# Ten filter units and most loads of the first spectra moved into the last turns of stage 1, in a three-stage graph-network kernel on one Trainium2 core

## What is computed

```python
h = relu(layernorm(x))                                   # layer 0
x = x + relu((norm_adj @ h) @ W.T + b)
h = relu(layernorm(x))                                   # layer 1
c = relu(bn1(conv1(h)))                                  # kernel width 1
c = bn2(conv2(c))                                        # width 17 along the nodes
x_conv = relu(c + h)
s = h @ w_se.T + b_se                                    # 3 features
A = exp(-|s_n - s_m|^2) * adj
x_nmp = A @ relu(h @ w_msg.T + b_msg)
x = x + GRU([x_conv, x_nmp], h)                          # three gates
```

## Time and profile before

| | us |
|---|---|
| median of 3 runs | 1807.17 (1806.46 to 1809.41) |
| the profiled execution's own time | 1806.71 |
| its span | 1804.9 |
| PE busy | 1770.6 (98%) |
| DVE, ACT, POOL busy | 1213.0, 997.1, 836.5 |

### The profile page before, as it was taken

The page is one execution under the profiler, slowest core; times in us unless marked ns, Lnnn a source line. Parts: engine busy times, 40 slices in busy tenths (PEclk is TensorE's granted clock), DMA queues, the critical chain, the costliest instruction groups (busy, mean ns, idle before and its releaser), DMA issues.

```text
span 1804.9 us, 29811 instructions
## 1 busy us (share of the span) xinstructions
PE 1770.6 (98%) x10214; PEld 1568.7 (87%) x10214; DVE 1213.0 (67%) x2306; ACT 997.1 (55%) x1781; POOL 836.5 (46%) x989
## 2 busy tenths in 40 slices
PE   6999999999999989999999999999999999999998
PEld 5999999999999979999988888888888888888887
DVE  7999999999999825555784544544544545545545
ACT  4888888888888866656542332332332332333322
POOL 5788888887777527656731221221221212212211
PEclk9999999999999999999999999999999999999999
DMA  6566566665555446676973435345345344344442
GB/s 205 173 197 221 197 212 206 201 221 189 200 193 189 153 132 147 166 174 158 226 202 101 85 102 121 81 103 123 78 107 118 77 113 104 87 117 89 101 110 42
DMA packets 513876, 262.56 MB, mean 145 GB/s; under 512 B 365639, under 2 KB 473543, under 8 KB 513726
## 3 DMA queue, kind: packets, MB, share of 16 engines
q1 hardware_dynamic: 513182, 260.58, 52.8%
q10 hardware_dynamic: 544, 0.07, 0.0%
HBM read 151.51 MB, written 109.05 MB: 144 GB/s over the span
## 4 chain that ended last, share of the span: by engine, by line
PE 94%; DVE 2%; issue 2%; POOL 1%; ACT 1%; DMA 0%; SPq 0%; ACTq 0%; DVEq 0%; POOLq 0%
PE P L113 70%; PE P L585 6%; PE P L912 5%; PE P L614 4%; PE P L654 4%; PE P L767 3%; PE P L633 1%; PE P L594 1%; DVE yo L792 0%; DVE wsum L730 0%; POOL axl L550 0%; DMA col<-in_cols 0%; DVE wh0l L742 0%; POOL af L547 0%; DMA yt<-y_d 0%
## 5 line engine op out<-in xcount | busy, mean ns | idle before, releaser
L894 POOL TENSOR_TENSOR xnx1l<-xnf,xnx1h 128x1024 fp32r<-128x1024 f32 x16 | 44.0, 2749 | 336.7 <-ACT xnx1h L887 336.7
L894 POOL TENSOR_TENSOR xnx0l<-xnf,xnx0h 128x1024 fp32r<-128x1024 f32 x15 | 41.6, 2772 | 317.7 <-ACT xnx0h L887 317.7
L1011 ACT ACTIVATE tr<-P,cold 128x512 f32<-128x512 f32 x64 | 44.2, 690 | 194.4 <-PE P L113 194.4
L1014 ACT ACTIVATE nn<-gn,col 128x512 f32<-128x512 f32 x64 | 46.4, 725 | 179.3 <-DVE gn L1035 179.3
L1044 DVE SCALAR_TENSOR_TENSOR tz<-tz,tr 128x512 f32<-128x512 f32 x63 | 43.6, 693 | 145.3 <-ACT tz L1025 145.2
L585 PE MATMUL P<-ah,hd 128*128 128x256 f32 x512 | 123.0, 383 | 12.2 <-ACT hd L383 12.2
L1025 ACT ACTIVATE tz<-P,cold 128x512 f32<-128x512 f32 x63 | 43.4, 689 | 159.6 <-PE P L113 159.6
L547 POOL TENSOR_TENSOR af<-af,at 128x512 f32<-128x512 f32 x64 | 111.0, 1735 | 42.1 <-ACT af L345 40.2
L1031 DVE SCALAR_TENSOR_TENSOR gn<-tr,gn 128x512 f32<-128x512 f32 x64 | 44.9, 701 | 127.3 <-ACT tr L1011 127.3
L550 POOL TENSOR_TENSOR axl<-af,axh 128x512 fp32r<-128x512 f32 x64 | 101.8, 1591 | 55.3 <-ACT axh L363 55.3
L585 PEld LDWEIGHTS P<-ah,hd 128*128 128x128 f32 x512 | 93.8, 192 | 22.7 <-ACT hd L383 12.2
(11 more groups left out here) (200 smaller groups left out, 6402.1 us busy)
## 6 DMA issues: line engine op xcount, KB each, us to landing
xh_d<-xst SPq DMA_DIRECT2D x64, 320.0 KB, 4.5
xl<-xh_d SPq DMA_DIRECT2D x40, 512.0 KB, 6.3
y_d<-yo SPq DMA_DIRECT2D x80, 256.0 KB, 2.5
x<-in_x SPq DMA_DIRECT2D x64, 256.0 KB, 2.7
a<-in_adj SPq DMA_DIRECT2D x64, 256.0 KB, 3.0
at<-in_adjt SPq DMA_DIRECT2D x64, 256.0 KB, 4.2
x_d<-x SPq DMA_DIRECT2D x64, 256.0 KB, 4.5
xn_d<-xt SPq DMA_DIRECT2D x64, 256.0 KB, 4.3
```

The lines of the kernel that those rows point to most:

```text
L894: e.e.tensor_tensor(o[1][:, :, :], xnf[p % 2][:, :, :, :].rearrange("p c i t -> p c (i t)"), o[0][:, :, :], ALU.subtract).then_inc(done, 1)
```

## The change

- PE: units 0 to 9 go into turns 66 to 69: unit 0, 2 and 4 at the end of turns 66, 67 and 68, units 1, 3 and 5 ahead of `dist` in turns 67, 68 and 69, units 6 to 9 at the end of turn 69. Units 0 to 5 share bank AG, each waits for the copy of the one before; from unit 6 on banks 4 to 7 are used as before. DVE makes the ten copies (a new semaphore `wevd`), ACT the others.
- ACT: from turn 66 on `h` comes right behind `msh` instead of behind `xst`. In the passage `xh0h` comes one unit's copy earlier, behind unit 20's.
- SP: the store of a group's spectra is cut by halves of the bins first (a, b) and then by channel, with a semaphore for each half (`sxa0`, `sxa1`, `sxb0`, `sxb1`), and stands ahead of the other stores of its turn. The last group's two a stores are issued in turn 71, its two b stores in turn 72. Four loads of the first 15 of 16 groups, for bin pairs 0 to 3, are issued at the end of turn 68; four small ones for the last group at the end of turn 71, once the a stores have landed.
- `first_stage_done` no longer waits for `sxb1`; ACT and DVE do that a little later (`last_spectra_stored`).
- The buffers `xs`, `a_` and `eye2` are placed where `xl` will lie, so that the early loads overwrite only what turn 68 no longer reads.

Three `nm_d` stores now come behind the four large loads. The diff, cut to its core:

```diff
         def first_sync(e, i):
             ...
                 load_adjt(e, i)
+
+            if live(i, 11, NB - 4):
+                store_spectra(e, i - 11)
+            if NB + 7 <= i < NB + 9:
+                for n in range(2):
+                    store_spectra(e, NB - 4 + 2 * (i - NB - 7) + n)
             ...
-            if live(i, 11, NB):
-                g, c, r = (i - 11) // 4, (i - 11) % 4 // 2, (i - 11) % 2 * NF
         ...
         def first_scalar(e, i):
             ...
+            if i >= NB + 2 and live(i, 6):
+                relu(e, i - 6)
             ...
+            if i < NB + 2 and live(i, 6):
+                relu(e, i - 6)
         ...
         def first_vector(e, i):
             ...
+            for n in UNITS_BEHIND.get(i - 1, ()):
+                unit_out(e, n)
             if live(i, 5):
             ...
                 t.then_inc(S["uv"], 1)
+            for n in UNITS_INSIDE.get(i, ()):
+                unit_out(e, n)
         ...
+        ONE_BANK, EARLY = 6, 10
+        UNITS_INSIDE = {NB + 3: (1,), NB + 4: (3,), NB + 5: (5,)}
+        UNITS_BEHIND = {NB + 2: (0,), NB + 3: (2,), NB + 4: (4,), NB + 5: (6, 7, 8, 9)}
         def filter_unit(e, n):
             ...
-            e.wait_ge(S["wev"], n - 3)
+            if n < ONE_BANK:
+                e.wait_ge(S["aglo"], NB)
+                e.wait_ge(S["wevd"], n)
+            else:
+                for name in ("aglo", "uvf", "xxlo", "tcm0", "tcm1"):
+                    e.wait_ge(S[name], NB)
+                units_out(e, max(n - 3, ONE_BANK))
         ...
+        def load_first_spectra(e):
+            for name in ("x2", "hd", "deg0", "ah"):
+                e.wait_ge(S[name], NB)
+            e.wait_ge(S["sxa0"], 32 * (NG // 2))
+            e.wait_ge(S["sxa1"], 32 * (NG // 2 - 1))
+            for q in range(2):
+                load_groups(e, q, 0, NG - 1)
+        def load_last_spectra(e):
+            e.wait_ge(S["sxa1"], 32 * (NG // 2))
+            for q in range(2):
+                load_groups(e, q, NG - 1, NG)
         ...
+                if i == NB + 4:
+                    load_first_spectra(e)
+                if i == NB + 7:
+                    load_last_spectra(e)
             first_stage_done(e)
-            for q in range(2):
-                load_spectra(e, q)
         ...
-            for n in range(UNITS):
-                if n == UNITS - 4:
+            for n in range(EARLY, UNITS):
+                if n == UNITS - 5:
                     first_stage_done(e)
                     spectra_hi(e, 0)
                 unit_out(e, n)
             ...
             spectra_hi(e, 1)
+            last_spectra_stored(e)
         ...
             weights_lo(e, 0)
+            last_spectra_stored(e)
             weights_sum(e, 1)
         ...
-            for n in range(UNITS + AHEAD):
+            for n in range(EARLY, UNITS + AHEAD):
                 filter_unit(e, n)
```

More of the change, by code:

```diff
@@ L121 @@
 out0 u x2 sx20 sx21 st1 ag1a ag1 rs1 n1b xn xnt xt sxt xxhi xxlo s uvf uvh uv cm0 cm1 tcm0 tcm1 h1 mshi mslo
-dist af am axhi axlo nmp nm snm dft0 dft1 xe0 xe1 sxh0 sxh1
-unit yz wev lxh0 lxh1 xsum xhi xlo wsum whi wlo frq com mt ye sy0 sy1 sy2 sy3
+dist af am axhi axlo nmp nm snm dft0 dft1 xe0 xe1 sxa0 sxa1 sxb0 sxb1
+unit yz wev wevd lxh0 lxh1 xsum xhi xlo wsum whi wlo frq com mt ye sy0 sy1 sy2 sy3
 lwg0 lwg1 lwg2 lwg3 lwg4 lwg5 wghi wg ly0 ly1 ly2 lxn0 lxn1 lnm0 lnm1 nmhi nmlov nmlop xnhi xnlov xnlop
@@ L195, in gnn_kernel @@
         xx = p1.hl("xx", [128, 512])
+        p1.at = spectra_at = keep.at + 40960
+        xs = [p1(f"x{i}", [128, 2, 256]) for i in range(5)]
+        a_ = [p1(f"a{i}", [128, 2, 256]) for i in range(2)]
+        eye2 = p1("eye2", [128, 512])
+        at = [p1(f"at{i}", [128, 512]) for i in range(7)]
+        x2 = [p1(f"x2{i}", [128, 2, 256]) for i in range(2)]
         stage = Place(nc, p1.at)
@@ L270, in load_adjt, with store_spectra @@
                 S[f"lat{b % 2}"], 16)
+        def store_spectra(e, k):
+            g, c, r = k // 4, k % 2, k % 4 // 2
+            e.wait_ge(S[f"xe{c}"], 4 * g + 4)
+            e.e.dma_start(xh_d[g][:, c, 16 * r * NF:16 * (r + 1) * NF],
+                          xst[g % 2][:, c, r * NF:(r + 1) * NF, :].rearrange("p r t -> p (r t)")).then_inc(
+                              S[f"sx{'ab'[r]}{g % 2}"], 16)
         def first_sync(e, i):
@@ L309, in spectrum_out, with relu @@
             e.wait_ge(S[f"dft{c}"], b + 1)
-            e.wait_ge(S[f"sxh{g % 2}"], 64 * (g // 2))
+            for half in "ab":
+                e.wait_ge(S[f"sx{half}{g % 2}"], 32 * (g // 2))
             e.e.copy(dst, src).then_inc(S[f"xe{c}"], 1)
+        def relu(e, b):
+            e.wait_ge(S["tcm0"], b + 1)
+            e.wait_ge(S["tcm1"], b + 1)
+            e.wait_ge(S["dft1"], b - 1)
+            e.e.activation(h1[b % 2][:, :, :], tcm[:, :, 0:256], ACT.Relu).then_inc(S["h1"], 1)
         def first_scalar(e, i):
@@ L577, in first_tensor @@
                 t.then_inc(S["nmp"], 1)
+            for n in UNITS_INSIDE.get(i, ()):
+                filter_unit(e, n)
             if live(i, 2):
@@ L635, in first_tensor @@
                 t.then_inc(S["xnt"], 1)
+            for n in UNITS_BEHIND.get(i, ()):
+                filter_unit(e, n)
         def unit_parts(n):
@@ L666, in unit_out @@
                 dst = wf[part % 2][:, :, c, 7 * j0:7 * (j0 + turns)].rearrange("p r (m o) -> p m r o", m=turns)
-                src = P[4 + n % 4][:, 0:140 * turns].rearrange("p (m r o) -> p m r o", m=turns, r=20)
+                src = P[unit_bank(n)][:, 0:140 * turns].rearrange("p (m r o) -> p m r o", m=turns, r=20)
             else:
                 dst = wf[part % 2][:, :, c, 7 * j0:256]
-                src = P[4 + n % 4][:, 0:140].rearrange("p (r o) -> p r o", r=20)[:, :, 0:parts(j0)]
-            e.e.copy(dst, src).then_inc(S["wev"], 1)
+                src = P[unit_bank(n)][:, 0:140].rearrange("p (r o) -> p r o", r=20)[:, :, 0:parts(j0)]
+            if n < EARLY:
+                e.e.tensor_copy(dst, src).then_inc(S["wevd"], 1)
+            else:
+                e.e.copy(dst, src).then_inc(S["wev"], 1)
         AHEAD = 4
@@ L684, in units_in, with load_groups, spectra_loaded @@
             return range(first + n * m // 18, first + n * (m + 1) // 18)
+        def load_groups(e, q, first, end):
+            for c in range(2):
+                e.e.dma_start(xl[q % 2][:, 16 * c + first:16 * c + end, :],
+                              xh_d[first:end, :, c, 64 * q:64 * q + 64].rearrange("g p r -> p g r")).then_inc(
+                                  S[f"lxh{q % 2}"], 16)
+        def load_first_spectra(e):
[9 more added lines that the diff above has]
+                load_groups(e, q, NG - 1, NG)
         def load_spectra(e, q):
-            for n in range(2):
-                e.wait_ge(S[f"sxh{n}"], 64 * (NG // 2))
+            for name in ("sxa0", "sxa1", "sxb0", "sxb1"):
+                e.wait_ge(S[name], 32 * (NG // 2))
             e.wait_ge(S["xhi"], 2 * q - 2)
             e.wait_ge(S["xlo"], 2 * q - 2)
[L692 to L695, removed]
+            load_groups(e, q, 0, NG)
+        def spectra_loaded(e, f):
+            e.wait_ge(S[f"lxh{f // 2 % 2}"], 32 * (f // 4 + 2))
         def bin_of(f):
```

34 lines of the change are left out of this document (16 added, 18 removed).

## The result

| | before | changed |
|---|---|---|
| median, us | 1806.99 (6 runs, 1805.34 to 1809.41) | 1797.49 (6 runs, 1795.71 to 1797.74) |
| span of the profiled execution | 1804.9 | 1794.6 |

The ratio is 0.9948, interval 0.9939 to 0.9958: faster by 0.5%. The forecast was 1797.5.

The account below looks back on a forecast made before the run. PE was taken to bound the kernel (94% of the chain). Unit 10 earlier (-0.8), 21.19 to 13.5 us of units (-7.6) and the wait (-1.1) sum to -9.5 us: 1797.5 forecast, own range 1796.4 to 1801, with rivals 1795.8 to 1802.0.

Parts of the forecast that it names:

- unit 10: First unit left in the passage after stage 1: starts at 663.0 us with POOL's allowance, against 663.76 before.
- 56 matmuls: PE's units left between stage 1 and stage 2: 13.5 us, where 86 matmuls took 21.19.
- The slots: PE's idle slots in turns 67 to 69: units 0 to 5 mostly fit, turn 69's `dist` about 0.4 us later.
- the gap: PE's 3.13 us idle ahead of the last `nmp`: four units, 2.9 us, hide wholly there.
- the clock: PE's clock behind the last `nmp` stays up; before, low clock cost 1.08 us in `dft` and 0.2 in `nmp`'s tail.
- the wait for `wh0l`: PE's wait ahead of stage 2: 1.38 us becomes 0.3, by 0.4 from ACT catching up and 0.7 from less overlap.
- POOL beside the copies: Turn 69's chain: DVE's unit copies slow POOL by 0.1 us, bounds 0 and 2 x 0.5.
- The moved `h`: ACT's earlier `h` from turn 66 on: ends `tcm`'s 4.43 us wait but doesn't shrink the turn, counted as nothing.
- Rival 1: Early loads delay turn 69's `nm_d` store and so the last `nmp`: 1797.5 to 1800.5 us, chance 12%.
- Rival 2: Last group's small loads land late, `xh0h` starts at 677 instead of 671, some 4 us reach PE: 1801.5, chance 8%.
- Rival 3: Units lengthen turns 67 to 69 instead of filling slots, 4.3 us in all: 1801.8 us, chance 6%.
- Rival 4: SP's new store order delays ACT's copies in 53 turns; at 0.3 us a turn 1813 us, slower, chance 3%.

Follow-up runs that it names:

- e4: Changed kernel with units 6 to 9 back behind stage 1, so PE's gap ahead of the last `nmp` stays open: 1804.01 us, ratio 0.9988.
- e10: e4 plus twelve throw-away matmuls behind turn 69's `dft`, whose results are never read: 1800.07 us, ratio 0.9968.
- e5: Changed kernel with POOL's `xsum` of the second bin pair waiting for DVE's first `wh0l`: 1796.37 us, ratio 0.9941.
- e3: Changed kernel with ACT's `h` back at its old place behind `xst` in all turns: 1798.51 us, ratio 0.9957.
- e2: Changed kernel with all ten units back behind stage 1, early loads and the rest kept: 1806.02 us, ratio 1.0002.
- e7: Changed kernel with the four large loads issued at the end of turn 70 instead of 68: 1803.55 us, ratio 0.998.
- e1: Changed kernel with the loads back behind `first_stage_done`, units staying in turns 66 to 69: 1804.04 us, ratio 0.9987.
- e8: Kernel before with only SP's order changed, each turn's spectra store ahead of its other stores: 1806.91 us, ratio 1.0.
- e11: Changed kernel once more, unaltered: 1796.75 us, ratio 0.9952 against the kernel before.
- e9: Changed kernel with twelve units moved instead of ten, and `xsum` of bin pair 1 behind `wh0l`: 1795.91 us, ratio 0.9938.

## Why the prediction was right

The steps (us). The forecast's times count in the trace of before; taking off that trace's 621.10, and 619.84 from the measured ones, sets both at the `dist` of turn 65:

| step | forecast | measured |
|---|---|---|
| `dist` of turn 69, later by | 0.40 | 0.22 |
| last `nmp`, counted from turn 65's `dist` | 39.30 | 39.26 |
| last `nmp` to unit 10 | 2.5 | 2.60 |
| unit 10, earlier by | 0.8 | 0.80 |
| 56 matmuls | 13.5 | 13.52 |
| wait ahead of stage 2 | 0.3 | 0.77 |
| stage 2, earlier by | 9.5 | 9.08 |

- **The slots, the gap and the clock** came as forecast. In turn 69 two small errors cancel: `dist` came 0.18 us earlier than forecast, and the chain from it to the last `nmp` took 4.89 us, not 4.75. The clock's share was argued from one slow `dft`; e4 and e10 measure it alone as 1.6 us, where the working had 1.08 + 0.2 + 0.5 = 1.8.
- **The mis-sized term is the wait for `wh0l`**: "most of that overlap goes: 0.7" was only 0.50 us of `wh0l`'s length (2.23 to 1.73), and PE's wait fell by 0.61 in all instead of 1.08. `xsum` starts 3.5 us behind `xh0h` in both traces, but `wh0h` 2.96 us behind it instead of 2.48, so `xsum` gained only half a microsecond on `wh0l`. The other piece, 0.4 for ACT catching up before unit 25, was 0.1: `wh0h` starts 2.29 us ahead of the end of PE's units (675.22) instead of 2.17 (684.95). e5 takes the whole overlap away (1.00 us of `wh0l` instead of the forecast's 0.7) and so gets the wait of 0.26 that I had put here, though ACT caught up by less.
- **POOL beside the copies, 0.1**: not needed. `axl` took 1.27 us at 657.57, right beside DVE's four copies (2.74 us from 656.54), and 1.28 at 642.38 with no copy beside it. The rule of the prediction held: the copies read PSUM, and POOL didn't feel them. The same section of the Trainium skill (SBUF — State Buffer, "Who interferes with whom") says that a DVE instruction with two SBUF inputs does contend with a GpSimd instruction that reads SBUF. The trace agrees: `wh0l` reads two tensors in SBUF, and beside `xsum` it lost half a microsecond.
- **The moved `h`, nothing**: the edit alone lengthens the passage by 0.34 us when undone (e3). I had asked what it gains against before, and not what the units would cost without it: part of its worth stood unseen in the slots' term.
- **Rival 1** (`nm_d` behind the loads): the delay was real, 3.7 us to landing instead of 2.0, and larger than forecast. Counted from turn 65's `dist` the store landed at 38.0, where the forecast's 658.5 is 37.4 and its 659.6, the latest time that costs nothing, is 38.5. So 0.5 of the 1.1 us of slack were left. In e2 the same store took 4.8 us, and ACT's `nm` copy did wait for it, by 0.30 us, which PE's wait for `axl` covered. The sign was near, and the forecast's account of it holds by half a microsecond.
- **Rival 2**: the small loads were issued at 665.36 and landed within 1.9 us, so `xh0h` didn't wait. Its mechanism is real, and its price was too small: e7 has `xh0h` 4.2 us late and pays 5.4 us, since the wait of PE was followed by a low clock, there and in e1.
- **Rival 3**: by turn 69's `dist` the turns with units had grown by 0.2 us together. **Rival 4**: e8 shows 0.00 us a turn.
- **The total.** The medians differ by 9.5 us and the passage by 9.08. The start-up alone moves single executions by over a microsecond, so there is luck in 1797.49 for 1797.5 (the same kernel gave 1796.75 in e11, 8.7 less than the kernel before beside it); 9.08 for 9.5 is what the working is to be held against. The lower end of the range's own sum, 1797.5 less 1.0, is 1796.5 and not 1796.4, which changes nothing.

## What to carry to other kernels

When work is moved into idle slots of the bounding engine, ask whether what that engine needs next comes early enough too: here units alone gave 2.3 us, loads alone 0.2, both 9.1. Price a gap of PE as its length and the slow matmuls behind it, and test the second part with matmuls whose results nobody reads. Compare two executions between two points around the edit: for the changed kernel that repeated to 0.03 us and for the kernel before and e8 to 0.16, while totals move by more than a microsecond at the start. Then look at the total all the same: in e4 and e1 part of what the passage gained was gone by the end.

## What the hardware showed that I had not expected

- **The start-up's clock differs between executions of the same code.** From 20 to 30 and 30 to 40 us the granted clock was 0.97 to 1.00 and then 0.83 to 0.86 in before, e2, e3, e4 and e9 (first `dist` at 41.7 to 42.1), 0.83 and 1.00 in e1, e5, e8 and e10 (40.4 to 41.1), and 1.00 in both in the changed kernel, e7 and e11 (40.6 to 40.7). The clock of these two stretches isn't the whole of it, since the earliest first `dist` of all, e5's 40.42, has the second pattern. Which it is doesn't follow the edits: e8 and before, e3 and e11 are on different sides.
- **The clock's price was not the same behind each wait.** Behind the gap of 3.30 us ahead of `nmp` (e4) the lower level cost 1.6 us; behind waits of 3.75 us (e7) and 4.64 us (e1) in the row of units it cost 2.5 and 3.1. I had priced those waits as waits alone. The low stretch was also longer there: the clock is 0.50 from about 661.2 to 664.5 in e4, from 677 to 683.5 in e1 and from 674 to 680.5 in e7, where the first 1.7 us of it passed while PE still idled. Two stretches of e7:

```profile
675.00:680.00 5.00, 4.33 (x18) 4.33 (x19) 1.74 (x2) 4.84 (x10) 3.56 (x2) 0.50 0.27 103
680.00:685.00 5.00, 5.00 (x41) 5.00 (x40) 2.41 (x3) 3.41 (x5) 1.91 (x1) 0.93 0.08 31
```

Whether the length of the wait or the work around it decides is not shown: both differ between these runs.
- **A store behind four loads of 256-byte pieces lands late.** The loads hold SP's queue for 7.61 us at 644.53 (7.86 in the kernel before, so that was expected), and the `nm_d` store behind them took 3.7 us to land here and in e11, and 4.8 in e2, instead of 2.0.
